# Seven slots a tile instead of eight in the first attention of layer 1

## The chip, the cores and the metric

The kernel runs as one program on one core of a Trainium2 chip. The time is that of the device in microseconds (us). PE is the tensor engine (matrix products into PSUM), ACT the scalar engine, DVE the vector engine, POOL the GpSimd engine, SP the engine that here only issues transfers. Each has its own instruction stream, works it off in order, and waits for the others by semaphores.

## The reference, cut to what matters

Two layers on 2 sequences of 2048 tokens of width 256. The change is in one stage, the first attention of layer 1: 16 query heads of 16 elements, 4 key and value heads, each token looking 128 tokens to both sides.

```python
Q = (x @ Wq.T).reshape(B, S, HKV, G, HEAD_DIM)
K = (x @ Wk.T).reshape(B, S, HKV, HEAD_DIM)
V = (x @ Wv.T).reshape(B, S, HKV, HEAD_DIM)
offs = jnp.arange(W) - WIN            # W = 257, WIN = 128
...
scores = jnp.einsum('bskgd,bswkd->bskgw', Q, K_win) * scale
attn = jax.nn.softmax(scores, axis=-1)
out = jnp.einsum('bskgw,bswkd->bskgd', attn, V_win)
return out.reshape(B, S, HQ * HEAD_DIM) @ Wo.T
...
h = _layernorm(x, axis=-1) * (1 + ca) + sa
x = x + ga * _L1_attn_ref(h, ...)
```

## The kernel before

The stage (`windowed_attention`) works on 32 tiles of 128 tokens, 16 of each sequence. A tile attends to itself and its two neighbours: three key tiles, two at the ends of a sequence. It is a software pipeline written out by hand. Each of PE, ACT and DVE has a function `step(s)` for s from -2 to 34, and in it a loop over `k`, the slots; the placement of each piece of work at a slot is the order of that engine's stream. In step s the pieces belong to different tiles:

- For tile s+2: normalise (ACT), turn the input (PE, `turn_input`), modulate (ACT), project to queries, keys and values (PE, `project`), copy the tokens of the queries out of PSUM (ACT, `copy_tokens`), then those of keys and values (DVE, `copy_key_tokens`), turn the queries (PE, `turn_queries`), copy them (ACT, `copy_queries`), turn and copy the keys (`turn_keys`, `copy_keys`).
- For tile s: the plain scores, 16 products (one a query head) of 32 rows by up to 384 columns, two a slot, called a pair. DVE takes of each, with the mask added, the maximum over the keys (`maxima`), and puts it into a spare column of the query tokens.
- For tile s-1: the query tokens with the maxima are turned again (`turn_maxima`), copied (`place_maxima`), and the turned scores, 4 products of 32 rows by 512 columns for each key tile, come out of PE with the maxima already taken off. ACT makes exponentials of them (`exps`), POOL cuts off what lies outside the window (`keep_inside`), and `values` multiplies with the values, four products side by side for each key tile.
- For tile s-2: the last values, then copy, reciprocal of the sums by logarithm and exponential. For tile s-3: `divide`, a transfer that packs the result (`pack_output`, SP), `project_out` (PE) and `add_output` (DVE).

Products of 32 rows use one of the array's four row groups each: the two plain ones of a slot go to two groups, the two turned ones to the other two. All of a slot's four are issued together.

PSUM has eight banks here: three for the plain scores (`PLAIN`), three for the turned (`TURNED`), one for the values, and one, `psm`, that projection, both kinds of turning and the output projection share in turn. At the head of a slot PE waits until the maxima (`maxima_done`) and exponentials (`exps_done`) have freed the banks that the slot writes. The sharing of `psm` gives other waits: `project_out` waits for the token copies of tile s+2 (`s_qtok`, `s_v`), and `turn_queries` of tile s+2 for `add_output` of tile s-3 (`s_x`), besides the copies. `spin` is idle products (128 by 128) that keep PE working in the first steps.

## Time and profile before

| | us |
|---|---|
| runs shown, median (lowest to highest of 3) | 3380.25 (3372.17 to 3385.89) |
| profiled execution, its own time | 3348.76 |
| its span | 3347.0 |
| first to last plain score product | 1210.9 to 1738.3 |
| PE, DVE, ACT busy, share of span | 95%, 58%, 47% |

The span is what the trace covers; the time contains 1.8 us around it. A row of the timeline gives start, length, engine, line, operation, output and inputs, and, in brackets, how long the engine sat idle before it and what released it. A product in 32 bits shows as two records, so two products are "x4". The granted clock is a share of TensorE's full 2.4 GHz.

### The profile page before, as it was taken

What the parts mean: (1) busy time and instruction counts of PE and PEld (TensorE: products, weight loads), DVE (VectorE), ACT (ScalarE), POOL (GpSimd) and SP (SyncE); (2) the same over time, 40 slices, a digit from 0 to 9 for tenths busy, and PEclk for the clock granted to TensorE, in tenths of its full rate; (3) what the DMA queues carried; (4) which work ended last, traced back from release to release, by engine and by line L of the source; (5) the groups of instructions that cost most, each with busy time, mean ns of one, the idle gap of its engine ahead of it and who ended that gap; (6) DMA issues with size and microseconds to landing.
All of it is one profiled execution on the core that took longest, in us unless ns stands there. A gap on an engine that the chain in (4) does not pass through costs nothing. (4 is left out here: it accounts for less than half of the span.)

```text
span 3347.0 us, 46661 instructions
## 1 busy us (share of the span) xinstructions
PE 3171.7 (95%) x15444; PEld 1840.2 (55%) x15445; DVE 1947.6 (58%) x4735; ACT 1567.5 (47%) x3527; POOL 709.6 (21%) x847
## 2 busy tenths in 40 slices
PE   8899999999999989999989999998999999998999
PEld 4455555555666653333326666665555666665555
DVE  6999995551111146666656788783224777775322
ACT  5666662212222236666665666663123566564211
POOL 1000003550000035555532223220001111111111
PEclk9999999999999999999999999999999999999999
DMA  9800004013111121111000000000001000000000
GB/s 332 283 1 1 0 1 157 27 52 99 44 45 45 39 78 29 29 29 29 22 18 32 10 10 8 10 5 28 0 0 35 10 10 8 10 7 4 13 13 26
DMA packets 114142, 134.01 MB, mean 40 GB/s; under 512 B 14451, under 2 KB 100231, under 8 KB 113675
## 3 DMA queue, kind: packets, MB, share of 16 engines
q1 hardware_dynamic: 105930, 109.45, 10.1%
q0 software_dynamic: 7872, 21.77, 2.1%
q8 instruction: 117, 1.92, 0.2%
q14 instruction: 95, 0.77, 0.1%
q10 hardware_dynamic: 128, 0.10, 0.0%
HBM read 60.22 MB, written 60.83 MB: 36 GB/s over the span
## 5 line engine op out<-in xcount | busy, mean ns | idle before, releaser
L1799 DVE CUSTOM_DVE_ANT_0 sb_win_masked<-ps_win_pss,sb_win_around 128x384 f32<-128x384 f32 (+1 forms) x512 | 256.3, 538 | 176.9 <-PE ps_win_pss L1927 176.8
L2436 PE MATMUL ps_loc_psa<-sb_stk_w,sb_loc_hT 128*128 128x512 f32 x768 | 351.0, 607 | 2.7 <-ACT sb_loc_hT L2192 2.7
L2225 ACT ACTIVATE sb_loc_pr<-ps_loc_psw,sb_loc_nb,sb_loc_sc 128x256 f32<-128x256 f32 x512 | 281.0, 568 | 119.2 <-DVE sb_loc_nb L2357 119.2
L1927 PE MATMUL ps_win_pss<-sb_win_kT,sb_win_q 32*128 32x384 f32 (+1 forms) x1024 | 231.0, 522 | 36.0 <-DVE sb_win_qtok L1799 34.0
L1661 ACT ACTIVATE sb_win_pT<-ps_win_pst 128x512 f32<-128x512 f32 x368 | 199.7, 595 | 125.4 <-PE ps_win_pst L1938 123.5
L2667 ACT ACTIVATE sb_mlp_gl<-ps_mlp_ps,sb_stk_col 128x512 f32<-128x512 f32 x96 | 65.9, 687 | 375.0 <-PE ps_mlp_ps L2756 374.7
L2436 PEld LDWEIGHTS ps_loc_psa<-sb_stk_w,sb_loc_hT 128*128 128x128 f32 x768 | 142.2, 192 | 179.6 <-issue 179.6
L2712 DVE SCALAR_TENSOR_TENSOR sb_mlp_hid<-ps_mlp_ps,sb_stk_col,sb_mlp_gl 128x512 f32<-128x512 f32 x96 | 71.5, 749 | 287.9 <-ACT sb_mlp_gl L2667 287.9
L747 PE MATMUL ps_rec_psp<-sb_rec_hT,sb_rec_w 128*128 128x512 f32 x512 | 231.9, 596 | 0.8 <-DVE sb_keep_modf L502 0.8
L1938 PE MATMUL ps_win_pst<-sb_win_qm,sb_win_kT 32*128 32x512 f32 x736 | 212.1, 649 | 1.5 <-ACT sb_win_pT L1661 0.8
L2138 POOL TENSOR_TENSOR sb_loc_t<-sb_loc_t 128x512 f32<-128x512 f32 x64 | 81.3, 1271 | 619.7 <-DVE sb_loc_t L2306 619.7
L1350 DVE TENSOR_TENSOR sb_exp_hid<-ps_exp_ps,sb_exp_act_f 128x512 f32<-128x512 f32 x71 | 49.1, 692 | 278.9 <-PE ps_exp_ps L1384 278.9
L1584 POOL TENSOR_SCALAR_AFFINE_SELECT sb_win_pT<-sb_win_pT 128x512 f32<-128x512 f32 x240 | 146.5, 634 | 247.2 <-ACT sb_win_pT L1661 247.2
L2756 PE MATMUL ps_mlp_ps<-sb_mlp_hT,sb_stk_w 128*128 128x512 f32 (+1 forms) x384 | 166.7, 625 | 22.3 <-DVE sb_mlp_hid L2712 22.3
L2764 PE MATMUL ps_mlp_pso<-sb_stk_w,sb_mlp_hid 128*128 128x256 f32 (+1 forms) x768 | 173.1, 382 | 7.0 <-DVE sb_mlp_hid L2712 7.0
L2353 DVE TENSOR_REDUCE sb_loc_top<-ps_loc_psw 128x4 f32<-128x1024 f32 x128 | 156.2, 1220 | 35.2 <-PE ps_loc_psw L2477 35.2
L1927 PEld LDWEIGHTS ps_win_pss<-sb_win_kT,sb_win_q 32*128 32x128 f32 x1024 | 81.2, 183 | 167.4 <-DVE sb_win_qtok L1799 161.7
L2764 PEld LDWEIGHTS ps_mlp_pso<-sb_stk_w,sb_mlp_hid 128*128 128x128 f32 (+1 forms) x768 | 143.3, 189 | 38.9 <-issue 10.5
L747 PEld LDWEIGHTS ps_rec_psp<-sb_rec_hT,sb_rec_w 128*128 128x128 f32 x512 | 97.7, 193 | 120.0 <-issue 119.6
L2756 PE MATMUL ps_mlp_ps<-sb_stk_hT,sb_stk_w 128*128 128x512 f32 (+1 forms) x384 | 155.5, 598 | 1.9 <-PEq L2089 1.9
L1556 POOL DMA_INDIRECT sb_win_got<-expert_results,sb_keep_row x64 | 62.2, 972 | 440.1 <-POOLq L1282 425.0
L1330 ACT COPY sb_exp_hidT<-ps_exp_psh 128x512 f32<-128x512 f32 x71 | 41.5, 585 | 232.7 <-PE ps_exp_psh L1392 232.7
(354 smaller groups left out, 6640.1 us busy)
## 6 DMA issues: line engine op xcount, KB each, us to landing
sorted_tokens<-sb_rec_blank SPq DMA_DIRECT2D x9, 4224.0 KB, 30.4
sb_exp_rows<-sorted_tokens SPq DMA_DIRECT2D x71, 128.0 KB, 2.0
expert_results<-sb_exp_res SPq DMA_DIRECT2D x71, 128.0 KB, 1.7
sb_moe_w_in<-in_L_ffn_w_in_eDF SPq DMA_DIRECT2D x8, 512.0 KB, 10.7
sb_moe_w_sw<-in_L_ffn_w_swiglu_eDF SPq DMA_DIRECT2D x8, 512.0 KB, 10.6
sb_exp_w_out<-in_L_ffn_w_out_eFD POOLq DMA_DIRECT2D x8, 512.0 KB, 8.9
sb_stk_angles<-in_angles SPq DMA_DIRECT2D x32, 128.0 KB, 3.8
sb_stk_xs_b<-sb_stk_y SPq DMA_DIRECT2D x64, 63.5 KB
```

The source lines that it names most:

```text
L747: i = nc.tensor.matmul(out, w[:, k, j * REC + g * P:j * REC + (g + 1) * P], hT[:, G % 2, k], start=(k == 0), stop=(k == KD - 1))
L1584: nc.gpsimd.affine_select(part, part, [[0, AG], [-towards, P]], ALU.is_ge, outside, base=0, channel_multiplier=towards).then_inc(s_cut, 1)
L1661: nc.scalar.activation(pT[:, n % PARTS], pst[:, n % TURNED], ACT.Exp, scale=SC).then_inc(s_e, 1)
L1799: nc.vector.tensor_tensor_reduce(masked[:, pair % 2, j, 0:keys], pss[:, (n + j) % PLAIN, 0:keys], around[:, first:first + keys], 1.0, -3e3 ...
L1927: nc.tensor.matmul(pss[:, n % PLAIN, 0:len(keys) * P], q[rows, u % RINGS, g], kT[rows, keys[0]:keys[-1] + 1].rearrange("p a n -> p (a n)") ...
L1938: nc.tensor.matmul(pst[:, n % TURNED], kT[rows, key], qm[rows, u % 2].rearrange("p g n -> p (g n)"), start=True, stop=True, skip_group_che ...
L2138: nc.gpsimd.tensor_tensor(qq, qq, t2[:, 0:INNER], ALU.add).then_inc(s_rope, 1)
L2225: e = nc.scalar.activation(pr[:, hf, h], psw[:, hf, h // 2, h % 2 * 256:h % 2 * 256 + 256], ACT.Exp, scale=sc8[:, b, hh:hh + 1], bias=nb[: ...
L2353: nc.vector.tensor_reduce(top[:, hf], psw[:, hf].rearrange("p a (h n) -> p (a h) n", h=2), AX_X, ALU.max).then_inc(s_top, 1)
L2436: t = nc.tensor.matmul(psa[:, c], hT[:, b, k, 1 - k:P + 1 - k], w[:, k, c * 512:(c + 1) * 512], start=(k == 0), stop=(k == KD - 1))
L2756: i = nc.tensor.matmul(ps[at:at + M, q % 2, i2], w1[:, k, i2 * HID + f * P:i2 * HID + f * P + M], hT[b][:, k], start=(k == 0), stop=(k == ...
L2764: i = nc.tensor.matmul(pso[:, t], hid[0:M, b, f, t * P:(t + 1) * P], w2[0:M, f], start=(f == 0 and t % 2 == 0), stop=(f == KH - 1 and t % ...
```

## The change

- A step has seven slots instead of eight. The plain scores have four banks of PSUM, one more, and the turned ones two, one less: `PLAIN, TURNED = 4, 2`.
- The first slot issues the plain pairs 0 and 1, four products on four row groups; slot k after it pair k+1. DVE takes the maxima in the same grouping. The turned scores and their exponentials of tile s-1 begin in slot 1 instead of 2.
- On PE `project`, `project_out`, `turn_queries`, `turn_keys` stand a slot earlier. On ACT `modulate` stands a slot later (2), `copy_queries` one earlier (5), `invert_sums` at 6; `copy_tokens` stays at 4. On DVE `copy_keys` is at 6; `copy_key_tokens` and `add_output` stay at 4.
- The values of the second key tile of tile s-1 move from slot 7 of step s to slot 0 of step s+1.
- The idle products are 5 a slot in steps -2 and -1 and none in step 0, instead of 8 a slot in all three.

```diff
-    PLAIN, TURNED = 3, 3
+    PLAIN, TURNED = 4, 2
...
-        SLOTS_PER_UNIT = AH // 2
+        SLOTS_PER_UNIT = AH // 2 - 1
...
+        def pairs_of(k):
+
+            return (0, 1) if k == 0 else (k + 1,)
...
-                        if k == 1 and s + 2 < NT:
+                        if k == 2 and s + 2 < NT:
                             modulate(s + 2)
                         if k == 3 and 0 <= s - 2 < NT:
                             copy_output(s - 2)
...
                         if k == 4 and s + 2 < NT:
                             copy_tokens(s + 2)
-                        if k == 6 and s + 2 < NT:
+                        if k == 5 and s + 2 < NT:
                             copy_queries(s + 2)
-                        if 0 <= s - 1 < NT and 0 <= k - 2 < 2 * len(key_tiles(s - 1)):
-                            exps(s - 1, k - 2)
+                        if 0 <= s - 1 < NT and 0 <= k - 1 < 2 * len(key_tiles(s - 1)):
+                            exps(s - 1, k - 1)
...
                         if k == 4 and s + 2 < NT:
                             copy_key_tokens(s + 2)
-                        if k == 7 and s + 2 < NT:
+                        if k == 6 and s + 2 < NT:
                             copy_keys(s + 2)
...
                         if 0 <= s < NT:
-                            maxima(s, k)
+                            for pair in pairs_of(k):
+                                maxima(s, pair)
...
-                        turned = 0 <= s - 1 < NT and 0 <= k - 2 < 2 * len(key_tiles(s - 1))
-                        if s <= 0:
-                            spin(nc, ident, pst[:, TURNED - 1], 8)
+                        turned = 0 <= s - 1 < NT and 0 <= k - 1 < 2 * len(key_tiles(s - 1))
+                        if s < 0:
+                            spin(nc, ident, pst[:, TURNED - 1], 5)
...
+                        if k == 0:
+                            for pair in plain:
+                                scores(s, pair, 0)
+                                scores(s, pair, 1)
                         for j in range(2):
-                            if 0 <= s < NT:
-                                scores(s, k, j)
+                            if k and plain:
+                                scores(s, plain[0], j)
                             if turned:
-                                scores_turned(s - 1, k - 2, j)
+                                scores_turned(s - 1, k - 1, j)
                         if k == 0 and 0 <= s - 1 < NT:
                             turn_maxima(s - 1)
+                        if k == 0 and 0 <= s - 2 < NT:
+                            values(s - 2, 1)
                         if k == 1 and s + 2 < NT:
                             turn_input(s + 2)
                         if k == 2 and 0 <= s - 2 < NT and len(key_tiles(s - 2)) == 3:
                             values(s - 2, 2)
-                        if k == 3 and s + 2 < NT:
+                        if k == 2 and s + 2 < NT:
                             project(s + 2)
-                        if k == 4 and 0 <= s - 3 < NT:
+                        if k == 3 and 0 <= s - 3 < NT:
                             project_out(s - 3)
+                        if k == 4 and s + 2 < NT:
+                            turn_queries(s + 2)
                         if k == 5 and s + 2 < NT:
-                            turn_queries(s + 2)
-                        if k == 6 and s + 2 < NT:
                             turn_keys(s + 2)
                         if k == 6 and 0 <= s - 1 < NT:
                             values(s - 1, 0)
-                        if k == 7 and 0 <= s - 1 < NT:
-                            values(s - 1, 1)
```

How the moved pieces stand to each other is seen in the streams. In PE's stream of an inner step before, between the projection (L1887) and the turning of the queries (L1898), with the output projection (L1980) between; plain scores are L1927, turned ones L1938:

```order
L1887 MATMUL ps_win_psm<-sb_win_wqkv,sb_win_hT 128x384 [waits rec_a]
L1887 MATMUL ps_win_psm<-sb_win_wqkv,sb_win_hT 128x384
L1927 MATMUL ps_win_pss<-sb_win_kT,sb_win_q 128x384 [waits rec_lnv,rec_tr]
L1938 MATMUL ps_win_pst<-sb_win_qm,sb_win_kT 128x512
L1927 MATMUL ps_win_pss<-sb_win_kT,sb_win_q 128x384
L1938 MATMUL ps_win_pst<-sb_win_qm,sb_win_kT 128x512
L1980 MATMUL ps_win_psm<-sb_win_wog,sb_win_oT 128x256 [waits rec_l,rec_back,rec_new,route_settle]
L1980 MATMUL ps_win_psm<-sb_win_wog,sb_win_oT 128x256
```

PE keeps this order in itself: project, one slot of scores, output projection, one slot of scores, queries turned. The semaphores carry names of an earlier stage whose numbers they reuse: rec_l and rec_back are `s_qtok` and `s_v`. Now, with all lines some higher (L1932 and L1943 are the scores, L1985 the output projection, L1903 the turning of the queries):

```order
L1932 MATMUL ps_win_pss<-sb_win_kT,sb_win_q 128x384 [waits rec_lnv,rec_tr]
L1943 MATMUL ps_win_pst<-sb_win_qm,sb_win_kT 128x512
L1932 MATMUL ps_win_pss<-sb_win_kT,sb_win_q 128x384
L1943 MATMUL ps_win_pst<-sb_win_qm,sb_win_kT 128x512
L1985 MATMUL ps_win_psm<-sb_win_wog,sb_win_oT 128x256 [waits rec_l,rec_back,rec_new,route_settle]
L1985 MATMUL ps_win_psm<-sb_win_wog,sb_win_oT 128x256
L1932 MATMUL ps_win_pss<-sb_win_kT,sb_win_q 128x384 [waits rec_lnv,rec_tr]
L1943 MATMUL ps_win_pst<-sb_win_qm,sb_win_kT 128x512
L1932 MATMUL ps_win_pss<-sb_win_kT,sb_win_q 128x384
L1943 MATMUL ps_win_pst<-sb_win_qm,sb_win_kT 128x512
L1903 MATMUL ps_win_psm<-sb_keep_ident,sb_win_qtok 128x128 [waits rec_oT,route_xadd,rec_back,rec_l]
```

These scores are those of slot 3 and slot 4; before, the same two waits stood behind the scores of slots 4 and 5. On ACT the copy of the query tokens (L1645, now L1649) stands behind the exponentials (L1661, now L1665) of slot 3 in both programs. Before, and then now:

```order
L1661 ACTIVATE sb_win_pT<-ps_win_pst 128x512 [waits rec_stats,rec_rstd] x2
L1645 COPY sb_win_qtok<-ps_win_psm 128x16x16 [waits rec_xn,rec_lu]
L1661 ACTIVATE sb_win_pT<-ps_win_pst 128x512 [waits rec_stats,rec_rstd] x4
L1653 COPY sb_win_q<-ps_win_psm 128x512 [waits rec_hT,rec_ec]
L1661 ACTIVATE sb_win_pT<-ps_win_pst 128x512 [waits rec_stats,rec_rstd] x2
```

```order
L1665 ACTIVATE sb_win_pT<-ps_win_pst 128x512 [waits rec_stats,rec_rstd] x2
L1649 COPY sb_win_qtok<-ps_win_psm 128x16x16 [waits rec_xn,rec_lu]
L1665 ACTIVATE sb_win_pT<-ps_win_pst 128x512 [waits rec_stats,rec_rstd] x2
L1657 COPY sb_win_q<-ps_win_psm 128x512 [waits rec_hT,rec_ec]
L1665 ACTIVATE sb_win_pT<-ps_win_pst 128x512 [waits rec_stats,rec_rstd] x4
```

On ACT only the copy of the queries has moved here. The exponentials above the token copy are, now as before, those of the turned scores that PE issues in its slot 3.

## Rows read from the trace of the kernel before

**Rows 1.** A stretch: busy PE, PEld, DVE, ACT, POOL; PEclk; DMA share; GB/s

```profile
1400.00:1500.00 100.00, 94.34 (x587) 33.85 (x585) 60.01 (x241) 65.91 (x138) 54.17 (x82) 0.98 0.12 31
```

**Rows 2.** Timeline of PE: one inner step and a half

```profile
1394.97 0.66 PE L1947 MATMUL ps_win_psm<-sb_keep_ident,sb_win_qtok 128*128 128x128 f32 x4
...
1400.87 1.56 PE L1887 MATMUL ps_win_psm<-sb_win_wqkv,sb_win_hT 128*128 128x384 f32 x4
1402.36 0.58 PE L1927 MATMUL ps_win_pss<-sb_win_kT,sb_win_q 32*128 32x384 f32 x1
...
1403.43 1.13 PE L1980 MATMUL ps_win_psm<-sb_win_wog,sb_win_oT 128*128 128x256 f32 x4
1404.49 0.58 PE L1927 MATMUL ps_win_pss<-sb_win_kT,sb_win_q 32*128 32x384 f32 x1
...
1405.57 0.66 PE L1898 MATMUL ps_win_psm<-sb_keep_ident,sb_win_qtok 128*128 128x128 f32 x4
1406.40 0.56 PE L1927 MATMUL ps_win_pss<-sb_win_kT,sb_win_q 32*128 32x384 f32 x1 [0.18 <-DVE sb_win_qtok L1799]
...
1407.73 1.06 PE L1963 MATMUL ps_win_pso<-sb_win_pT,sb_win_v 128*32 128x512 f32 x8
...
1410.80 0.92 PE L1927 MATMUL ps_win_pss<-sb_win_kT,sb_win_q 32*128 32x384 f32 x4
1411.64 0.66 PE L1947 MATMUL ps_win_psm<-sb_keep_ident,sb_win_qtok 128*128 128x128 f32 x4
1412.50 0.91 PE L1927 MATMUL ps_win_pss<-sb_win_kT,sb_win_q 32*128 32x384 f32 x4 [0.20 <-DVE sb_win_qtok L1799]
1413.34 0.44 PE L1881 MATMUL ps_win_psm<-sb_keep_ident,sb_win_xn 128*128 128x128 f32 x2
1414.40 0.88 PE L1927 MATMUL ps_win_pss<-sb_win_kT,sb_win_q 32*128 32x384 f32 x1 [0.62 <-DVE sb_win_qtok L1799]
...
1416.38 1.80 PE L1963 MATMUL ps_win_pso<-sb_win_pT,sb_win_v 128*32 128x512 f32 x8
...
1429.95 0.66 PE L1947 MATMUL ps_win_psm<-sb_keep_ident,sb_win_qtok 128*128 128x128 f32 x4
```

**Rows 3.** Timeline of ACT in the same step

```profile
1402.47 0.37 ACT L1645 COPY sb_win_qtok<-ps_win_psm 128x256 f32<-128x256 f32 x1 [0.42 <-PE ps_win_psm L1887]
...
1405.66 1.08 ACT L1661 ACTIVATE sb_win_pT<-ps_win_pst 128x512 f32<-128x512 f32 x2 [1.05 <-PE ps_win_pst L1938]
...
1416.46 1.09 ACT L1661 ACTIVATE sb_win_pT<-ps_win_pst 128x512 f32<-128x512 f32 x2 [1.84 <-PE ps_win_pst L1938]
```

**Rows 4.** Timeline of DVE in the same step

```profile
1403.01 0.21 DVE L1783 COPY sb_win_v<-ps_win_psm 128x64 f32<-128x64 f32 x1
1403.57 0.56 DVE L1799 CUSTOM_DVE_ANT_0 sb_win_masked<-ps_win_pss,sb_win_around 128x384 f32<-128x384 f32 x1 [0.34 <-PE ps_win_pss L1927]
...
1404.60 0.42 DVE L1816 TENSOR_TENSOR sb_keep_x<-ps_win_psm,sb_keep_x 128x256 f32<-128x256 f32 x1
```

**Rows 5.** The page's group of the exponentials

```profile
L1661 ACT ACTIVATE sb_win_pT<-ps_win_pst 128x512 f32<-128x512 f32 x368 | 199.7, 595 | 125.4 <-PE ps_win_pst L1938 123.5
```

**Rows 6.** Timeline of ACT near the stage's end

```profile
1731.13 1.09 ACT L1661 ACTIVATE sb_win_pT<-ps_win_pst 128x512 f32<-128x512 f32 x2 [0.44 <-PE ps_win_pst L1938]
```

**Rows 7.** Timeline of PE, the first steps, and the slot that follows rows 6

```profile
1202.53 0.38 PE L1881 MATMUL ps_win_psm<-sb_keep_ident,sb_win_xn 128*128 128x128 f32 x2
...
1210.88 0.70 PE L1927 MATMUL ps_win_pss<-sb_win_kT,sb_win_q 32*128 32x256 f32 x4
...
1225.88 0.91 PE L1927 MATMUL ps_win_pss<-sb_win_kT,sb_win_q 32*128 32x384 f32 x4 [0.61 <-DVE sb_win_qtok L1799]
...
1731.87 0.45 PE L1927 MATMUL ps_win_pss<-sb_win_kT,sb_win_q 32*128 32x256 f32 x1 [0.77 <-ACT sb_win_pT L1661]
```

**Rows 8.** Stretches of later stages, columns as in rows 1

```profile
2270.00:2280.00 10.00, 6.33 (x44) 5.54 (x44) 3.50 (x7) 7.32 (x21) 1.04 (x1) 0.73 0.02 4
...
3160.00:3170.00 10.00, 6.29 (x18) 2.08 (x17) 7.18 (x36) 4.34 (x8) 0.00 (x0) 0.95 0.01 2
```

More of the change, by code:

```diff
@@ L1720, in step @@
                             log_sums(s - 2)
-                        if k == 7 and 0 <= s - 2 < NT:
+                        if k == 6 and 0 <= s - 2 < NT:
                             invert_sums(s - 2)
@@ L1726, in step @@
                             lead_rows()
-                        if k == 7 and s == NT + 1:
+                        if k == 6 and s == NT + 1:
                             pack_last_output()
@@ L1839, in step @@
                             lead_statistics()
-                        if k == 7 and s == NT:
+                        if k == 6 and s == NT:
                             lead_offsets()
@@ L1984, in step @@
                     for k in range(SLOTS_PER_UNIT):
-                        turned = 0 <= s - 1 < NT and 0 <= k - 2 < 2 * len(key_tiles(s - 1))
-                        if s <= 0:
-                            spin(nc, ident, pst[:, TURNED - 1], 8)
-                        if s == NT + 1 and k > 5 or s == NT + 2 and k < 2:
+                        turned = 0 <= s - 1 < NT and 0 <= k - 1 < 2 * len(key_tiles(s - 1))
+                        if s < 0:
+                            spin(nc, ident, pst[:, TURNED - 1], 5)
+                        if s == NT + 1 and k > 4 or s == NT + 2 and k < 2:
                             spin(nc, ident, pss[:, 0], 10)
-                        if 0 <= s < NT:
-                            maxima_done(s, k)
+                        plain = pairs_of(k) if 0 <= s < NT else ()
+                        for pair in plain:
+                            maxima_done(s, pair)
                         if turned:
-                            exps_done(s - 1, k - 2)
+                            exps_done(s - 1, k - 1)
+                        if k == 0:
+                            for pair in plain:
+                                scores(s, pair, 0)
+                                scores(s, pair, 1)
                         for j in range(2):
-                            if 0 <= s < NT:
-                                scores(s, k, j)
+                            if k and plain:
+                                scores(s, plain[0], j)
                             if turned:
-                                scores_turned(s - 1, k - 2, j)
+                                scores_turned(s - 1, k - 1, j)
                         if k == 0 and 0 <= s - 1 < NT:
                             turn_maxima(s - 1)
+                        if k == 0 and 0 <= s - 2 < NT:
+                            values(s - 2, 1)
                         if k == 1 and s + 2 < NT:
```

## The prediction

> **What bounds the kernel now.** I read the windows by stage first. In the stage of the change PE is busy 94.3 of 100 us, ACT 65.9, DVE 60.0, POOL 54.2, at a granted clock of 0.98 [rows 1]: PE sets the pace, the others have a third of the time to spare. Then PE's timeline, for the length of a step. From one turning of maxima (L1947) to the next there are 1411.64 - 1394.97 = 16.67 us; the step after has 18.31 [rows 2]. The steps come in these two lengths in the middle of the stage (four have 18.31), with a few of 14.2 to 16.4 where a tile has two key tiles or the stage begins or ends.
>
> A step is made of these pieces, from start to start [rows 2]. A slot of two plain and two turned products: 1405.57 - 1404.49 = 1.08. A slot of two plain ones alone: 1411.64 - 1410.80 = 0.84. Turning of queries or maxima 0.66, of the input 0.44 (0.27 until the next could start), projection 1.49, output projection 1404.49 - 1403.43 = 1.06, values of a key tile 1.06 (1.0 until the next starts). The idle places are short: 0.20 and 0.62 behind the plain slots, 0.18 behind the turned queries, all waiting for DVE's maxima. So before, each of the longer pieces on `psm` lies between its waits and what these wait for: PE projects, does a slot of scores, and by then the copies are made.
>
> Last I read ACT and DVE against the start of a PE slot, since the change moves PE against them. The slot that starts at 1404.49 gives ACT its first exponential at 1405.66, 1.17 later [rows 2, 3]. One exponential takes 0.60, a pair 1.09, so the second begins 0.49 after the first [rows 5, 6]. PE starts 0.74 after the start of the first when it waits for that one only (1731.87 - 1731.13) [rows 6, 7]. The slot of 1402.36 gives DVE its maxima at 1403.57, 1.21 later, and `add_output` follows at 1404.60, 1.03 after those began, and takes 0.42 [rows 2, 4].
>
> **The change, part by part.** What it gives: four plain products on four row groups in slot 0. Four with two of them longer (512 columns) take 1.08 in a slot, two alone 0.84 [rows 2]; I take 0.85 for the four, and 1.08 is the other end. That removes one plain slot, 0.84 a step, and the idle 0.20 and 0.62 behind such slots. POOL gets more time before the values of the second key tile, which before waited for nothing; moving them costs nothing.
>
> First cost: two turned banks. Each slot needs the two banks of the slot before, so both its exponentials. With three it waited for the first only. The shortest distance of two turned slots becomes 1.17 + 0.74 + 0.49 = 2.40, where before it was 1.17 + 0.74 = 1.91. What stands behind the waiting product on PE is everything, plain scores and `psm` work. Slots 1, 5 and 6 hold less work than that: 1.08 + 0.27, 1.08 + 0.26 (the keys) and 1.08 + 1.0. Slot 6 is followed by slot 0, which needs all four plain banks and so the maxima of the last pair: 1.21 + 1.03 + about 0.15 = 2.39. Three slots cost 2.4 each.
>
> Second cost: the output projection in slot 3 waits for the token copies, and ACT makes them in slot 4, behind the exponentials of PE's own slot 3. From the start of slot 3: exponentials at 1.17, the second issued by 1.66, the copy at about 2.14, 0.37 long; the copy of the values on DVE ends 1403.22 - 1402.47 = 0.75 after the token copy began [rows 3, 4], so at 2.89; with 0.15 for the semaphore 3.04. PE was done at 1.08: idle 1.96. Then 1.06. Slot 3 takes 4.1. Before, that wait stood a slot later and fell away under the scores.
>
> Third cost: `turn_queries` in slot 4 waits for `add_output`, which on DVE stands behind the maxima of slot 4. From the slot's start 1.21 + 1.03 + 0.42 + 0.15 = 2.81; PE was done at 1.08: idle 1.73. Then 0.66 to 0.72. Slot 4 takes 3.5. Before, the slot was a later one than that of `add_output`.
>
> The full step: slot 0 0.85 + 0.7 + 1.0 = 2.55; slot 1 2.4; slot 2 1.08 + 1.0 + 1.49 = 3.57; slot 3 4.1; slot 4 3.5; slot 5 2.4; slot 6 2.39. Together 20.9, against 16.67: 4.2 more. ACT's work (66% of a step of 16.7 is 11) and DVE's (10) have room in it. The packing transfer has about 4 us more than it needs before the added wait, and is no term. Steps 3 to 29 have both waits: 27 x 4.2 = 113, less 1 for tiles with two key tiles, 112. Steps 2, 30, 31 and 32 have only the slots of 2.4: together 6. Step 1 is even.
>
> The first steps gain. From the turning of tile 1's input (1202.53) to the first scores (1210.88) are 8.4 us, and step 0 takes 15.0 until 1225.88 [rows 7], both stretched by idle products. Followed by their own chain of copies, with the durations above, I get about 6.3 and 10.4; the step before gives 2 more. With 1 back for a lower clock where idle products are gone: -8, between -2 and -12.
>
> Then the clock. At 1414.40, behind the idle 0.20 and 0.62, the turned slot took 1416.38 - 1414.40 = 1.98 instead of 1.08, and the values 1.80 instead of 1.06 [rows 2]; that is the lower of the two levels, 1.2 GHz instead of 2.4, and it is the whole difference of 1.64 between the step lengths. ACT's exponentials began 2.06 after that slot's start instead of 1.17, 0.9 later [rows 2, 3]. The new step has idle places of 1.96 and 1.73 and about 1.05 twice, PE busy some 71%. Ten-microsecond stretches of later stages with PE busy 6.3 us: six, granted 0.73 in the first, 0.95 in the last, 0.87 in the mean [rows 8]. With 0.89 for 71%, a fifth of the time is at half clock, 4.6 us a step; at 0.9 to 1.64 for each 3.7 us as above that is 1.1 to 2.0 a step, and I take 1.4: 38, less the 4 x 1.64 = 7 that is there already, 31. Ends: -7 (no fall left) and two whole falls a step, 27 x 3.3 - 7 = 82.
>
> The Trainium skill bears on this term ("TensorE: Matmul & The Clock Gate", section "A second HAM failure mode: psum-queue depth-cycling"): frequent short idles of PE between groups of products, when it cycles through banks, make its clock go up and down between the two levels. The trace agrees at 1414.40 [rows 2]. Its section "HAM oscillation" speaks of long idle gaps only, and by that alone the term would be -7 and the time 38 us lower; rows 2 show a fall behind shorter ones.
>
> Sum: 112 + 6 - 8 + 31 = 141; I round down to 135 since waits take up part of a slow slot. Against the profiled 3348.76 that is 3484. That execution lies 31.5 below the median of the runs shown, 3380.25; added to the median, 3515. The same difference may not return, which the range takes in.
>
> **The rivals.** A: only the two turned banks cost, and the two `psm` waits are hidden after all. Slots 3 and 4 would then last 2.4 by the banks, the step 18.1, or 1.4 more; 27 x 1.4 + 6 - 8 + about 8 for the clock = 44, so 3424. For it speaks that before neither wait shows in the timeline; against it that both stand in the streams a slot earlier against copies that did not move. 6%.
>
> B, the other side: slot 0 does what it is for, and the exponentials are early enough. The step loses 0.84 and 0.62 of idle and keeps the rest, with the first steps' 8: -27 x 0.84 - 8 = -31, so 3349, and with the idle too 3333. It holds if ACT can begin the first exponential within about 0.7 of the slot's start, so that the slots stay at 1.91; rows 3 show 1.17, and this is a way through the array that the change does not touch. 4%.
>
> C: the clock stays low for most of a step. Then the slots last up to 0.9 longer each and the projections double: 27 x 3.3 to 27 x 5 for the clock instead of 38, so on the forecast's scale 3570 to 3615. For it: idle places of nearly 2 us in succession; against it: rows 8 are idler still and hold 0.87. 10%.
>
> **How the numbers follow.** Forecast 78%, C 10%, A 6%, B 4%, something unseen near no change 2%. Range 3450 to 3575: low end without any clock term (3380 + 103 = 3483) and with the 31 us of the profiled execution not returning; high end most of the clock's upper bound. Half a per cent, 17 us, is about what can be told from no change. Faster by more than that 4%, within it 3%, slower 93%.
>
> **What would show it.** Right: in the timeline after, the output projection sits idle about 1.9 us behind the copy of the values (DVE) and the turned queries about 1.7 behind `add_output`; slots 1, 5 and 6 are 2.4 apart with ACT or DVE as releaser; a step of about 21 to 23; the granted clock in the stage at 0.85 to 0.93; PE's share of it at 75% or less. Wrong: a step under 18, or these two waits missing, would throw out costs two and three; a clock of 0.98 the last term; slot 0 of more than 1.1 the gain.

## The result and the profile after

| us | before | after |
|---|---|---|
| median of the runs (lowest to highest of 4) | 3383.07 (3372.17 to 3388.05) | 3527.88 (3521.32 to 3530.92) |
| ratio, 95% interval | | 1.043 (1.0399 to 1.0461) |
| profiled execution, its own time | 3348.76 | 3521.32 |
| stage, first idle products to the next stage | 583.9 (1181.87 to 1765.74) | 729.7 (1212.61 to 1942.35) |
| of it: start to first turning of maxima (step 1) | 44.9 | 41.2 |
| of it: from there to the last turning (step 32) | 513.3 | 662.1 |
| of it: behind the last turning | 25.7 | 26.5 |
| everything behind the stage | 1581.3 | 1577.3 |

Four per cent slower; 3515 was forecast. The stage is 145.9 us longer and the medians are 144.8 apart, so all of it lies in the stage, and in its steps. (The stage begins 30.7 us later in the profile after, in code that did not change. That belongs to the execution that was profiled: it lies 34.3 below the median with before, 6.6 below with after.)

The windows first, columns as in rows 1; the kernel after:

```profile
1400.00:1500.00 100.00, 77.74 (x434) 26.11 (x426) 46.03 (x174) 48.07 (x99) 42.52 (x63) 0.83 0.08 20
1500.00:1600.00 100.00, 73.17 (x453) 26.16 (x457) 45.92 (x188) 52.50 (x110) 42.50 (x65) 0.94 0.09 23
1600.00:1700.00 100.00, 75.75 (x442) 25.97 (x434) 49.47 (x190) 48.14 (x102) 37.71 (x58) 0.90 0.09 24
1700.00:1800.00 100.00, 73.14 (x477) 25.18 (x479) 50.14 (x190) 52.68 (x108) 43.35 (x66) 0.97 0.08 20
```

PE was busy 94 of 100 us [rows 1] and is now busy 75, and its clock fell from 0.98 to 0.91 in the mean of these four. No other engine got busier. Here no engine is full: they wait for each other in a ring. The waits of PE between 1220 and 1900 us (engine, line, waited for: us in all, times, longest) say where:

```profile
PE ps_win_pss L1932 <- DVE sb_win_qtok L1803: 66.4, 81, 1.3
PE ps_win_psm L1985 <- DVE sb_win_v L1787: 51.5, 27, 1.9
PE ps_win_psm L1903 <- DVE sb_keep_x L1820: 42.5, 27, 1.6
```

L1985 is `project_out`, L1903 `turn_queries`, L1932 the plain scores at the head of a slot: the two `psm` waits 27 times each, as forecast, and three slots a step that wait for banks. One undisturbed step in PE's timeline (a slot begins with its first L1932):

```profile
1496.80 0.66 PE L1952 MATMUL ps_win_psm<-sb_keep_ident,sb_win_qtok 128*128 128x128 f32 x4
1497.39 1.06 PE L1968 MATMUL ps_win_pso<-sb_win_pT,sb_win_v 128*32 128x512 f32 x8
1498.39 0.58 PE L1932 MATMUL ps_win_pss<-sb_win_kT,sb_win_q 32*128 32x384 f32 x1
...
1500.78 0.56 PE L1932 MATMUL ps_win_pss<-sb_win_kT,sb_win_q 32*128 32x384 f32 x1 [0.88 <-DVE sb_win_qtok L1803]
...
1504.33 0.58 PE L1932 MATMUL ps_win_pss<-sb_win_kT,sb_win_q 32*128 32x384 f32 x1
...
1507.38 1.10 PE L1985 MATMUL ps_win_psm<-sb_win_wog,sb_win_oT 128*128 128x256 f32 x4 [1.91 <-DVE sb_win_v L1787]
1508.41 0.58 PE L1932 MATMUL ps_win_pss<-sb_win_kT,sb_win_q 32*128 32x384 f32 x1
...
1511.15 0.63 PE L1903 MATMUL ps_win_psm<-sb_keep_ident,sb_win_qtok 128*128 128x128 f32 x4 [1.59 <-DVE sb_keep_x L1820]
1511.71 0.58 PE L1932 MATMUL ps_win_pss<-sb_win_kT,sb_win_q 32*128 32x384 f32 x1
...
1514.10 0.56 PE L1932 MATMUL ps_win_pss<-sb_win_kT,sb_win_q 32*128 32x384 f32 x1 [0.99 <-DVE sb_win_qtok L1803]
...
1516.71 0.93 PE L1932 MATMUL ps_win_pss<-sb_win_kT,sb_win_q 32*128 32x384 f32 x8 [0.47 <-DVE sb_win_qtok L1803]
1517.57 0.66 PE L1952 MATMUL ps_win_psm<-sb_keep_ident,sb_win_qtok 128*128 128x128 f32 x4
```

From turning to turning 1517.57 - 1496.80 = 20.77, against 16.67 [rows 2]. By the starts, the turning and the values behind it take 1.59, slots 1 to 6 take 2.39, 3.55, 4.08, 3.30, 2.39 and 2.61, and the four products side by side of the next slot 0 take 0.86. Other steps take 22.8 and 24.8. This is why, in the step before:

```profile
1482.96 1.96 PE L1985 MATMUL ps_win_psm<-sb_win_wog,sb_win_oT 128*128 128x256 f32 x4 [1.91 <-DVE sb_win_v L1787]
...
1493.38 1.94 PE L1968 MATMUL ps_win_pso<-sb_win_pT,sb_win_v 128*32 128x512 f32 x8
1495.24 1.63 PE L1932 MATMUL ps_win_pss<-sb_win_kT,sb_win_q 32*128 32x384 f32 x8
```

The output projection takes 1.96 instead of 1.10, the values 1.94 instead of 1.06, the slot of four 1.63 instead of 0.93: the lower of the two levels, 1.2 GHz. It fell behind the idle 1.91, came back (the turned queries at 1488.37 take 0.63), and fell again.

The other end of the two new waits, ACT and DVE in the step above:

```profile
1505.50 1.09 ACT L1665 ACTIVATE sb_win_pT<-ps_win_pst 128x512 f32<-128x512 f32 x2 [1.58 <-PE ps_win_pst L1943]
1506.47 0.38 ACT L1649 COPY sb_win_qtok<-ps_win_psm 128x256 f32<-128x256 f32 x1
```
```profile
1507.02 0.21 DVE L1787 COPY sb_win_v<-ps_win_psm 128x64 f32<-128x64 f32 x1
...
1510.10 0.55 DVE L1803 CUSTOM_DVE_ANT_0 sb_win_masked<-ps_win_pss,sb_win_around 128x384 f32<-128x384 f32 x1
...
1510.58 0.42 DVE L1820 TENSOR_TENSOR sb_keep_x<-ps_win_psm,sb_keep_x 128x256 f32<-128x256 f32 x1
```

Slot 3 starts at 1504.33. ACT makes its exponentials from 1505.50 and only then, at 1506.47, the token copy; DVE's copy of the values ends at 1507.23, 2.90 after the slot's start (2.89 was reckoned), and PE starts 0.15 later. Slot 4 starts at 1508.41; `add_output` stands behind both maxima and ends at 1511.00, 2.59 after it, and PE starts 0.15 later.

### The profile page after: what moved, and what is told of

It reads as the page before. It is cut to its first block and busy times, and to the rows that moved or that the text cites. A ratio compares the mean times of both kernels' runs of the same rounds, so it can differ in the third digit from the quotient of the medians.

```text
span 3519.6 us, 46418 instructions
## 1 busy us (share of the span) xinstructions
PE 3187.3 (91%) x15322; PEld 1833.3 (52%) x15323; DVE 1941.8 (55%) x4735; ACT 1568.1 (45%) x3527; POOL 708.0 (20%) x847
## 5 line engine op out<-in xcount | busy, mean ns | idle before, releaser
L1665 ACT ACTIVATE sb_win_pT<-ps_win_pst 128x512 f32<-128x512 f32 x368 | 199.8, 594 | 269.9 <-PE ps_win_pst L1943 269.9
L1932 PE MATMUL ps_win_pss<-sb_win_kT,sb_win_q 32*128 32x384 f32 (+1 forms) x1024 | 224.9, 588 | 73.4 <-DVE sb_win_qtok L1803 66.4
L1943 PE MATMUL ps_win_pst<-sb_win_qm,sb_win_kT 32*128 32x512 f32 x736 | 228.1, 695 | 1.7 <-ACT sb_win_pT L1665 1.7
L1932 PEld LDWEIGHTS ps_win_pss<-sb_win_kT,sb_win_q 32*128 32x128 f32 x1024 | 78.3, 206 | 190.3 <-DVE sb_win_qtok L1803 158.1
L2363 DVE TENSOR_REDUCE sb_loc_top<-ps_loc_psw 128x4 f32<-128x1024 f32 x128 | 156.1, 1220 | 35.2 <-PE ps_loc_psw L2487 35.2
```

The lines of the kernel that those rows point to most:

```text
L1665: nc.scalar.activation(pT[:, n % PARTS], pst[:, n % TURNED], ACT.Exp, scale=SC).then_inc(s_e, 1)
L1932: nc.tensor.matmul(pss[:, n % PLAIN, 0:len(keys) * P], q[rows, u % RINGS, g], kT[rows, keys[0]:keys[-1] + 1].rearrange("p a n -> p (a n)") ...
L1943: nc.tensor.matmul(pst[:, n % TURNED], kT[rows, key], qm[rows, u % 2].rearrange("p g n -> p (g n)"), start=True, stop=True, skip_group_che ...
L2363: nc.vector.tensor_reduce(top[:, hf], psw[:, hf].rearrange("p a (h n) -> p (a h) n", h=2), AX_X, ALU.max).then_inc(s_top, 1)
```

## The experiments

They ran on three chips: e1 to e4 on one, c_again and e5 to e7 on the second, e8 to e10 on the third. Before takes 3347.9, 3348.8 and 3348.4 us there, so times can be set side by side within about 1 us. Those stated in the expectations of e1 to e4 are on the scale of the comparison above (before 3383, after 3528); read them as differences. "Clean step" is the length of a full step, three key tiles, without a fall of the clock. Step lengths, stages and granted clocks are each from one profiled execution.

### c_again: the kernel after, unchanged

> The changed kernel once more, beside the other kernels on the same chip. A ratio to the kernel before of about 1.043, as measured; on the chip of the runs above, where the kernel before took 3348, that is 3490.

Measured 3492.8 against 3348.8, ratio 1.0432 (1.0415 to 1.0449). The ratio is that of the comparison above, 1.043, though both kernels are some 35 us faster here. Stage 730.1; granted clock 0.92 from 1250 to 1790 us.

### e1_copies_early: the token copies a slot earlier

```diff
-                        if k == 4 and s + 2 < NT:
+                        if k == 3 and s + 2 < NT:
                             copy_tokens(s + 2)
...
-                        if k == 4 and s + 2 < NT:
+                        if k == 3 and s + 2 < NT:
                             copy_key_tokens(s + 2)
```

> The changed kernel, with the two token copies (copy_tokens on ACT, copy_key_tokens on DVE) a slot earlier, ahead of the exponentials and maxima of slot 3. My theory: the output projection then finds its copies ready about 1.0 us after the start of slot 3, so slot 3 falls from 4.07 to the 2.4 of two turned banks, 1.67 less in 27 steps = 45, and a few us of clock: about 3475 to 3482, a clean step of 19.1. Rival (the psm waits are no cost of their own, two turned banks explain the step): no change, 3528.

Measured 3446.2, ratio 1.0302 (1.0283 to 1.0321), 46.6 below c_again, of which 27 x 1.68 = 45 is the step. The wait of `project_out` is gone, that of `turn_queries` is untouched, and the step is 1476.73 - 1457.65 = 19.08:

```profile
1457.65 0.66 PE L1952 MATMUL ps_win_psm<-sb_keep_ident,sb_win_qtok 128*128 128x128 f32 x4
1466.25 1.13 PE L1985 MATMUL ps_win_psm<-sb_win_wog,sb_win_oT 128*128 128x256 f32 x4
1470.31 0.63 PE L1903 MATMUL ps_win_psm<-sb_keep_ident,sb_win_qtok 128*128 128x128 f32 x4 [1.59 <-DVE sb_keep_x L1820]
1476.73 0.66 PE L1952 MATMUL ps_win_psm<-sb_keep_ident,sb_win_qtok 128*128 128x128 f32 x4
```

So the order of ACT's and DVE's streams makes this wait, and nothing on PE. The clock did not get better: 0.91 from 1250 to 1790 us, with the other wait left, and steps of 21.1 and 22.5 among those of 19.1.

### e2_add_early: `add_output` ahead of the maxima of slot 4

```diff
+                        if k == 4 and 0 <= s - 3 < NT:
+                            add_output(s - 3)
                         if 0 <= s < NT:
...
-                        if k == 4 and 0 <= s - 3 < NT:
-                            add_output(s - 3)
```

> The changed kernel, with only add_output put ahead of the maxima in slot 4 on DVE. My theory: turn_queries waits no longer, slot 4 falls from 3.30 to 2.4, 0.9 less in 27 steps = 24, and some clock: about 3500, a clean step of 19.9. The rival says no change, 3528.

Measured 3452.9, ratio 1.0325 (1.0303 to 1.0348), 40 below c_again, where some 28 were expected. The clean step is 19.88 (1482.85 - 1462.97 below): 0.9 less than 20.76, since PE then waits 0.67 for its banks instead. More was gained than the 0.9 a step, 27 x 0.9 = 24: the steps of 22.8 and 24.8 went too, the longer ones are now 20.96 (one of 22.87 is left), and the clock is 0.95 in the stage instead of 0.92.

```profile
1462.97 0.66 PE L1952 MATMUL ps_win_psm<-sb_keep_ident,sb_win_qtok 128*128 128x128 f32 x4
1473.56 1.10 PE L1985 MATMUL ps_win_psm<-sb_win_wog,sb_win_oT 128*128 128x256 f32 x4 [1.91 <-DVE sb_win_v L1787]
...
1482.85 0.66 PE L1952 MATMUL ps_win_psm<-sb_keep_ident,sb_win_qtok 128*128 128x128 f32 x4
```

### e3_both_early: both edits

The two diffs above together.

> Both of the moves before. My theory: 2.57 less a step, 69 us, and about 10 to 15 of clock since PE is idle less: 3440 to 3455, a clean step of 18.2, still slower than the kernel before (3383). If two turned banks were all the cost, 3528; if the two waits were all of it, this would come out at or under 3383.

Measured 3390.4, ratio 1.0138 (1.0117 to 1.016), 102 below c_again, where 73 to 88 were expected. Clean step 18.18, which is 27 x 2.58 = 70; most of the rest is the clock, now 0.97, which was reckoned at 10 to 15. Neither long wait is left, and the kernel is still 1.4% slower than before. What is left:

```profile
1464.07 0.56 PE L1932 MATMUL ps_win_pss<-sb_win_kT,sb_win_q 32*128 32x384 f32 x1 [0.88 <-DVE sb_win_qtok L1803]
...
1472.41 0.56 PE L1932 MATMUL ps_win_pss<-sb_win_kT,sb_win_q 32*128 32x384 f32 x1 [0.67 <-DVE sb_win_qtok L1803]
...
1474.80 0.56 PE L1932 MATMUL ps_win_pss<-sb_win_kT,sb_win_q 32*128 32x384 f32 x1 [0.99 <-DVE sb_win_qtok L1803]
```

Slots of 2.39 (1472.41, 1474.80) wherever less work than that stands in one: with 0.47 at slot 0 and 0.19 at slot 4, 3.2 us idle a step, where rows 2 show 1.0.

### e4_banks_only: eight slots as before, banks as after

```diff
-    PLAIN, TURNED = 3, 3
+    PLAIN, TURNED = 4, 2
```

> The kernel before, eight slots, with nothing but the banks exchanged (four plain, two turned). My theory: slots of turned products last at least 2.4; of six in a step four are shorter than that now (2.1, 2.1, 1.9, 2.3) and lose 0.3, 0.25, 0.5, 0.1, while the idle 0.20 and 0.62 behind the plain slots goes; so about even, 16.9 a step, 3385 to 3400. Rival: the banks alone are the main cost of the change (slots of 2.4 wherever they stand), then about 1.4 a step, 3425.

Measured 3353.1, ratio 1.0019 (1.0009 to 1.0028). The full steps are 16.85 (1425.91 - 1409.06 below) and the clock is 1.00: none of the steps of 18.31 is left. In eight slots the exchange of banks costs 0.18 in a full step, some 5 us in all, and the falls that are gone give back 4 x 1.64 = 7. What stays is in the steps with less work in a slot: the last two take 16.0 and 16.7 where before has 15.3 and 14.1. The stage is 588.1 against 583.9.

```profile
1409.06 0.66 PE L1947 MATMUL ps_win_psm<-sb_keep_ident,sb_win_qtok 128*128 128x128 f32 x4
1413.26 0.56 PE L1927 MATMUL ps_win_pss<-sb_win_kT,sb_win_q 32*128 32x384 f32 x1 [0.26 <-DVE sb_win_qtok L1799]
...
1420.60 0.56 PE L1927 MATMUL ps_win_pss<-sb_win_kT,sb_win_q 32*128 32x384 f32 x1 [0.67 <-DVE sb_win_qtok L1799]
...
1425.91 0.66 PE L1947 MATMUL ps_win_psm<-sb_keep_ident,sb_win_qtok 128*128 128x128 f32 x4
```

Two turned banks alone are thus not the loss of e3; the loss is that seven slots with the same `psm` work each must be longer than 2.39 to hide it, and three of them hold less.

### e5_short_maxima: who releases a slot

```diff
-    nc.vector.tensor_tensor_reduce(masked[:, pair % 2, j, 0:keys], pss[:, (n + j) % PLAIN, 0:keys],
-                                   around[:, first:first + keys], 1.0, -3e38, ALU.add, ALU.max,
+    nc.vector.tensor_tensor_reduce(masked[:, pair % 2, j, 0:P], pss[:, (n + j) % PLAIN, 0:P],
+                                   around[:, first:first + P], 1.0, -3e38, ALU.add, ALU.max,
```

The maxima are taken over the first 128 keys alone, all else is as in the kernel after.

> The changed kernel with maxima taken over the first 128 of the keys only (the rest of the keys is left out of the maximum): each of DVE's maxima is about 0.27 shorter, ACT's exponentials as they were. The profile names DVE as the releaser of the slots of 2.39 and ACT alike. My theory: slots 1 and 5 wait for the second exponential on ACT, so they stay at 2.39 with ACT named; slot 4 (add_output behind two maxima) and slot 6 (slot 0 needs the last maxima) lose about 0.5 each: a clean step of 19.75. Rival: DVE's maxima are what the slots wait for: slots 1 and 5 fall to 1.9 too, a clean step under 19.

One execution, 3450.8, so only its timeline is used. DVE's two maxima together now take 0.5 instead of 1.0, and the slot is still 2.39 (1502.69 - 1500.30), released by ACT's second exponential:

```profile
1500.30 0.58 PE L1932 MATMUL ps_win_pss<-sb_win_kT,sb_win_q 32*128 32x384 f32 x1
...
1501.46 1.08 ACT L1665 ACTIVATE sb_win_pT<-ps_win_pst 128x512 f32<-128x512 f32 x2 [0.47 <-PE ps_win_pst L1943]
...
1501.72 0.29 DVE L1803 CUSTOM_DVE_ANT_0 sb_win_masked<-ps_win_pss,sb_win_around 128x128 f32<-128x128 f32 x1
...
1502.69 0.56 PE L1932 MATMUL ps_win_pss<-sb_win_kT,sb_win_q 32*128 32x384 f32 x1 [0.99 <-ACT sb_win_pT L1665]
```

The trace of after puts these waits down to DVE since maxima and exponentials end within 0.1 us there. Either alone would give nearly the same slot. The wait of `turn_queries` did shrink with the maxima, from 1.59 to 1.06. Clean step 19.70.

### e6_fill: idle products in the two long waits

```diff
+                        if k == 3 and 3 <= s and s + 2 < NT:
+                            maxima_done(s, 5)
+                            spin(nc, ident, pss[:, (s * AH + 10) % PLAIN], 15)
                         if k == 3 and 0 <= s - 3 < NT:
                             project_out(s - 3)
+                        if k == 4 and 3 <= s and s + 2 < NT:
+                            maxima_done(s, 6)
+                            spin(nc, ident, pss[:, (s * AH + 12) % PLAIN], 12)
                         if k == 4 and s + 2 < NT:
```

> The changed kernel with idle products (128 by 128) in its two long waits: 15 of about 0.11 us behind the scores of slot 3, 12 behind those of slot 4, into plain banks that are free then. They take 1.6 and 1.3 of the 1.9 and 1.6 us that PE would sit idle, so the wait itself stays. My theory (the excess of a step over 20.76 is TensorE's clock falling after idle places): the granted clock in the stage rises to 0.97 or more, nearly all steps are 20.8 to 21.2, some 25 to 29 us less than the changed kernel, ratio about 1.035. Rival: the falls have nothing to do with being idle, or idle products do not count as work: no change, 1.043. Other side: the idle products end too late and push, up to 0.3 a step, 8 us more.

Measured 3456.6, ratio 1.0315 (1.0299 to 1.033), 36 below c_again, where 25 to 29 were expected. Every full step is 20.77 (1488.59 - 1467.82), and the clock 1.00 from 1250 to 1790 us:

```profile
1467.82 0.66 PE L1952 MATMUL ps_win_psm<-sb_keep_ident,sb_win_qtok 128*128 128x128 f32 x4
1476.42 1.86 PE L114 MATMUL ps_win_pss<-sb_keep_ident 128*128 128x128 f32 x15
1478.40 1.10 PE L1985 MATMUL ps_win_psm<-sb_win_wog,sb_win_oT 128*128 128x256 f32 x4
...
1480.51 1.53 PE L114 MATMUL ps_win_pss<-sb_keep_ident 128*128 128x128 f32 x12
1482.17 0.63 PE L1903 MATMUL ps_win_psm<-sb_keep_ident,sb_win_qtok 128*128 128x128 f32 x4
1488.59 0.66 PE L1952 MATMUL ps_win_psm<-sb_keep_ident,sb_win_qtok 128*128 128x128 f32 x4
```

The ring is as long as ever and the falls are gone. So the waits set the step, and the idle in them cost a further 36 us by the clock.

### e7_spread: seven slots with the work laid out for them

```diff
-                        if k == 0 and 0 <= s - 2 < NT:
-                            values(s - 2, 1)
                         if k == 1 and s + 2 < NT:
                             turn_input(s + 2)
-                        if k == 2 and 0 <= s - 2 < NT and len(key_tiles(s - 2)) == 3:
-                            values(s - 2, 2)
+                        if k == 1 and 0 <= s - 2 < NT:
+                            values(s - 2, 1)
                         if k == 2 and s + 2 < NT:
                             project(s + 2)
-                        if k == 3 and 0 <= s - 3 < NT:
-                            project_out(s - 3)
-                        if k == 4 and s + 2 < NT:
+                        if k == 3 and s + 2 < NT:
                             turn_queries(s + 2)
-                        if k == 5 and s + 2 < NT:
+                        if k == 4 and s + 2 < NT:
                             turn_keys(s + 2)
+                        if k == 4 and 0 <= s - 2 < NT and len(key_tiles(s - 2)) == 3:
+                            values(s - 2, 2)
+                        if k == 5 and 0 <= s - 3 < NT:
+                            project_out(s - 3)
```

ACT and DVE follow: token copies at 3, `copy_queries` at 4, `copy_keys` and `copy_output` at 5, `add_output` at 6 ahead of the maxima. Since `psm` now goes from the turned keys to the output projection, `project_out` waits for `copy_keys` (`s_k`) in place of the token copies, and `turn_queries` for the `add_output` of one tile earlier.

> Seven slots and the changed kernel's banks, but the work on psm and the values placed so that each slot with turned products holds about 2.4 us and no wait ends late: slot 1 turns the input and takes the values of the second key tile, 2 projects, 3 turns the queries, 4 turns the keys and takes the values of the third, 5 projects out, 6 the values of the first; token copies at 3, copy_queries at 4, copy_keys and copy_output at 5, add_output at 6 ahead of the maxima. My theory: slots of 1.45, 2.42, 2.57, 2.4, 2.4, 2.4, 2.6, a step of 16.25 against 16.67, 0.4 less in 27 steps = 11, 4 less from the first steps, 3 more in the last: 8 to 18 us under the kernel before, ratio 0.995 to 0.998. Rival: with two turned banks no placement pays, since every slot carries the 0.49 of a second exponential: a step over 16.9, ratio 1.002 or more as in the exchange of banks alone.

Measured 3371.5, ratio 1.0064 (1.005 to 1.0078): the best with seven slots (e10 below is equal within its interval), and still slower than before. The clean step is 16.97 and not 16.25, the side of the rival ("over 16.9"). Slots 2 to 6 came as reckoned; the miss is at the head of a step:

```profile
1495.03 0.93 PE L1932 MATMUL ps_win_pss<-sb_win_kT,sb_win_q 32*128 32x384 f32 x8 [0.22 <-issue]
1495.89 0.66 PE L1952 MATMUL ps_win_psm<-sb_keep_ident,sb_win_qtok 128*128 128x128 f32 x4
1497.14 0.88 PE L1932 MATMUL ps_win_pss<-sb_win_kT,sb_win_q 32*128 32x384 f32 x2 [0.59 <-DVE sb_win_qtok L1803]
```

Four plain products fill all four plain banks at once. With the values moved out of slot 0, PE is ready for the next pair 1.5 after their start (1497.14 - 0.59 - 1495.03), and DVE has not yet taken the maxima of pair 0. The fourth bank buys nothing there.

### e10_spread_fill: e7 with idle products in the waits of slots 0 and 3

```diff
+                        if k == 0 and 1 <= s and s + 2 < NT:
+                            exps_done(s - 1, 0)
+                            spin(nc, ident, pst[:, groups_before(s - 1) * 4 % TURNED], 5)
...
+                        if k == 3 and 1 <= s and s + 2 < NT:
+                            maxima_done(s, 5)
+                            spin(nc, ident, pss[:, (s * AH + 10) % PLAIN], 5)
```

> The seven slots with the work spread, with 5 idle products in each of its two idle places (0.59 behind the turned maxima, where slot 1 waits for the maxima of pair 0, and 0.67 in slot 3). That kernel measured 1.0064 with clean steps of 16.97 and some 12 us of longer ones. My theory: the longer steps go, ratio 1.002 to 1.004; with 16.97 against 16.67 and tails of slots of 2.4 it stays over the kernel before. Rival: the clock was its whole deficit: ratio 0.998 or less.

Measured 3368.9, ratio 1.006 (1.0046 to 1.0073). A miss: 1.002 to 1.004 was expected, and the interval overlaps that of e7, so the totals show no gain. The clock is now 1.00 from 1250 to 1740 us and the stage is 605.5, against 583.9 before and 611.9 in e7. What separates it from before is 13 in the steps up to the 29th (27 x 0.3 = 8 of it the clean step), 7 in the last two (17.3 and 19.3 against 15.3 and 14.1), and 8 behind the last turning (33.6 against 25.7), less 6.5 up to the first turning. That the last part is longer because values and projection of the last tiles come later in their steps was not tested.

### e8_before_fill: the kernel before with idle products in its longest wait

```diff
                             turn_input(s + 2)
+                        if k == 1 and 1 <= s and s + 2 < NT:
+                            exps_done(s - 1, 0)
+                            spin(nc, ident, pst[:, groups_before(s - 1) * 4 % TURNED], 5)
```

> The kernel before, with 5 idle products (about 0.55 us) behind the turned input in slot 1, where PE sits idle 0.62 us for the maxima and behind which its clock fell in four steps. My theory: no step of 18.3 is left, 4 x 1.64 = 6 to 7 us less than the kernel before, ratio 0.998. Rival: the falls are at the mercy of the execution and these idle places too short to matter: no change. Other side: the idle products push the slot by 0.1 in 29 steps, 3 more.

Measured 3341.3, ratio 0.9981 (0.9972 to 0.999). Where rows 2 have the wait of 0.62, five idle products stand, and the full steps are 16.67 (1428.61 - 1411.95 = 16.66), with none of 18.31. In the profiled execution step 1, at the lower level already ahead of the first added products (granted clock 0.54 from 1226 to 1234 us), takes 20.2 instead of 15.7, so its stage is no shorter than before (583.1 against 583.9); the gain stands in the medians, 7.1 us:

```profile
1411.95 0.66 PE L1947 MATMUL ps_win_psm<-sb_keep_ident,sb_win_qtok 128*128 128x128 f32 x4
...
1413.92 0.71 PE L114 MATMUL ps_win_pst<-sb_keep_ident 128*128 128x128 f32 x5
...
1428.61 0.66 PE L1947 MATMUL ps_win_psm<-sb_keep_ident,sb_win_qtok 128*128 128x128 f32 x4
```

### e9_before_fill_few: e8 with the fewer idle products of the change in the first steps

```diff
-                        if s <= 0:
-                            spin(nc, ident, pst[:, TURNED - 1], 8)
+                        if s < 0:
+                            spin(nc, ident, pst[:, TURNED - 1], 5)
```

> The same, and the idle products of the first steps as in the changed kernel (5 a slot in steps -2 and -1, none in step 0). The profile of the changed kernel shows 3.7 less from the stage's start to its first turning of maxima, with seven slots; with eight I expect 3 to 8 less than the run without: ratio 0.996 to 0.9975.

Measured 3340.6, ratio 0.9975 (0.9965 to 0.9986): faster than before by a quarter of a per cent, and the best of all. The fewer idle products were expected to give 3 to 8 us; the medians of e8 and e9 are 0.7 apart and the intervals overlap, so the totals don't show that they give anything. The profiles do a little: the first turning comes at 1219.3 instead of 1225.6, the next step gives back 1.3 of it (21.53 against 20.19, both at the lower level), and the stage is 578.5 against 583.1.

## Why the prediction was right, and where its sizes were off

**The two added waits** were the largest term, and each came where and as long as the sum had it: 1.91 and 1.59 for 1.96 and 1.73, 27 times each. Their mechanism is shown from both sides: e1 takes one away by moving ACT's and DVE's copies, e2 the other by moving one DVE instruction, e3 both. With the clock that goes with them they are 102 of the 144 us. The method that found them was to add, from a slot's start on PE, what stands in front of the wanted instruction in another engine's stream; it gave 2.89 where the trace has 2.90. The second wait was over-reckoned by 0.14. Half of it is the two maxima, counted as 1.03 before the next instruction where it is 0.96 here (1510.58 - 1509.62); the other half is PE, which ends the slot's scores 1.15 after its start and not 1.08 (1511.15 - 1.59 - 1508.41).

**The two turned banks** gave slots of 2.39 where 2.4 was said. ACT's second exponential alone holds them there, as e5 shows. The term was right only as a part of this change. By itself the exchange costs 0.18 in a full step (e4). With seven slots and both waits gone (e3) the step is still 18.18 - 16.67 = 1.5 longer than before, because the work between the slots was not laid out again: e7, laid out, is back at 16.97.

**Slot 0** took 0.86 before the turning (0.85), and the slot ahead of it 2.61 instead of 2.39. The last maximum ends at 1516.35, and PE starts 0.36 later, where other releases take 0.15. Why is open: in e7 the same products start behind an idle of 0.22 that no semaphore explains (1495.03). Clean step: 20.9 predicted, 20.76 measured, with slot 4 at 3.30 for 3.5, slot 0 at 2.45 for 2.55 and slot 6 at 2.61 for 2.39, which partly make up for each other.

**The first steps** were the term most mis-sized: -8, within -2 to -12, with step 1 "even". Up to the first turning it is -3.7, and step 1 took 19.1 (1253.76 to 1272.90) against before's 15.7 (1226.72 to 1242.37), which gives it all back. What was sized wrong is the 1 us for a lower clock. Step 1 after has its waits where e1 has them, but its products take nearly twice as long; after, then e1:

```profile
1260.90 2.93 PE L1892 MATMUL ps_win_psm<-sb_win_wqkv,sb_win_hT 128*128 128x384 f32 x4
```
```profile
1223.35 1.56 PE L1892 MATMUL ps_win_psm<-sb_win_wqkv,sb_win_hT 128*128 128x384 f32 x4
```

e1 has the same few idle products, and its step 1 runs at a clock of 1.00 and takes 15.1. Up to its first turning e1 is 8.0 shorter than before, e2 6.6, e9 6.4, c_again only 2.4. So the gain reckoned from the copies can be had, but it differs from one profiled execution to the next, and in step 1 the clock takes it back: 0.71 there after, and 0.67 to 0.74 in c_again, e2, e3 and e9. What brings the clock down is open: e8, with all the idle products of before, has the low step 1 too.

**The clock** was reckoned at 38 in all, 31 net. Measured: filling the waits gave 36 in all (e6), which less the 7 that before has is 29 net. By the steps: 3 to 29 take 137.5 more than before, of which the clean step is 27 x 4.09 = 110, and 27 are left for the clock. The granted clock of 0.91 lies in the forecast 0.85 to 0.93, PE's share at the forecast 75%. The term was right in size, though I had reckoned it from falls behind idles of 0.2 and 0.6 [rows 2], and here it comes behind idles of 1.9; that the size came out is in part luck. By the Trainium skill ("TensorE: Matmul & The Clock Gate", "A second HAM failure mode: psum-queue depth-cycling") short idles between groups bring the clock down and up again. The trace agrees: 0.92 with the idles (c_again) and 1.00 with them filled (e6). But e4 has idles of 0.26, 0.19 and 0.67 in every step and a clock of 1.00, so short idles alone do not say when it falls.

**The sum** was 141 and was rounded down to 135, because slow slots swallow part of a wait; 144.8 was measured, and no run shows that the rounding was needed. By the terms: the clean step 110 (112 with the tiles of two key tiles), the other long steps 8.5 (6), the first steps nothing (-8), the clock 27 (31). The 8 that the first steps did not give and the 2.5 of the other long steps are in part made up by 6 less in the other two, and that is luck. The 31.5 added for the profiled execution is not part of the change: where before takes 3348.8, after takes 3492.8 (c_again), and the forecast on that scale is 3484. It belonged in the sum only because the comparison was run where before takes 3383.

**The rivals.** A (banks only, 3424) needed both waits hidden; both stand in the trace, and its step of 18.1 is e3's 18.18, reached only with two edits that take the waits away. B (the exponential within 0.7 of the slot's start) fell by 1505.50 - 1504.33 = 1.17. C (low clock most of the time) fell by the clock of 0.91.

So of 144 us: 102 go with the two waits, their falls of the clock included, that is 70 of step length and for the most part clock in the rest. The other 42 are what e3 still has over before: some 38 in steps 3 to 29, where slots hold less work than the banks need (27 x (18.18 - 16.67) = 41 if all steps were clean ones), and the rest at the stage's two ends.

## What to carry to other kernels

When a step on one engine moves by a slot, count again for each thing it waits for where that stands in the other engine's stream; a producer left where it was can turn hidden latency into a wait in every round (here two instructions, 102 us). A double buffer sets the least distance of its users to the latency plus both evacuations, here 2.39 us, so a slot must carry at least that much work, or it waits. Here even the layout made for that (e7) stayed above the kernel before. Where a wait of PE can't be removed, idle products into a free bank can keep the clock up; that was worth 36 us in the kernel after, behind waits of 1.9 and 1.6, and 7 us in the kernel before, the only gain over it that the runs show.

## What the runs showed of the hardware that I had not expected

- Filling waits with products whose result nobody reads held the clock at 1.00 without lengthening the step: 20.77 with 27 of them a step, 20.76 without (e6).
- Exchanging a turned bank for a plain one made the clock better: with waits of 0.26, 0.19 and 0.67 spread over the step (e4) the falls of before are gone, though PE is idle longer in a step (1.12 against the 1.00 of rows 2). Why these idles do no harm and the 0.20 and 0.62 of before do is open.
- From the end of a maximum on DVE to PE's start it took 0.15 us at slots 2 and 6 of the step shown, and 0.36 ahead of the four products of slot 0.
